# Two-layer graph network, first mixer's stage: GpSimd's row gathers issued in spells tied to TensorE's progress

## The reference

```python
xn = _layernorm(x, axis=-1)
x = x + _L0_gnn_ref(xn, sent_repr, src, dst, ...) + _L0_mix_ref(xn[None], W_qkv, W_out, b_out)[0]
```

## Time and profile before

| | us |
|---|---|
| timed executions | 2204.93, 2221.02, 2217.95 |
| median | 2217.95 |
| span of the profiled execution, first to last instruction | 2177.7 |
| median less span | 40.25 |

### The profile page before, as it was taken

How to read it: one execution, slowest core, us unless ns; L and a number is a source line. 1 busy time by engine, 2 the same in 40 slices (tenths; PEclk the granted TensorE clock), 3 DMA queues, 4 the chain that set the end, 5 groups by cost and what they waited for, 6 DMA issues and landing times. The chain is left out here.

```text
span 2177.7 us, 31463 instructions
## 1 busy us (share of the span) xinstructions
PE 1591.3 (73%) x7770; PEld 1251.9 (57%) x7770; DVE 1251.5 (57%) x3879; ACT 862.1 (40%) x2965; POOL 1067.5 (49%) x1173
## 2 busy tenths in 40 slices
PE   5635577766756786969999766877788887875892
PEld 4533444444444455959999654655566655664792
DVE  3523555555556687855777635454455455676435
ACT  2221656656555786635777431000011000143451
POOL 3751666666666500421222156666666666326351
PEclk8755668667777898989999867888888888896896
DMA  6741544444444302836555133333333333122786
GB/s 193 223 138 40 150 121 126 127 131 126 123 123 142 108 18 84 260 111 203 180 171 179 62 89 106 90 93 91 88 91 88 92 90 93 52 93 85 219 264 223
DMA packets 176882, 276.92 MB, mean 127 GB/s; under 512 B 28920, under 2 KB 132218, under 8 KB 176456
## 3 DMA queue, kind: packets, MB, share of 16 engines
q0 software_dynamic: 50352, 136.58, 21.8%
q1 hardware_dynamic: 82194, 94.23, 14.2%
q10 hardware_dynamic: 44166, 44.14, 6.1%
HBM read 202.35 MB, written 73.58 MB: 127 GB/s over the span
## 5 line engine op out<-in xcount | busy, mean ns | idle before, releaser
L501 POOL DMA_INDIRECT ring<-feat_d,src_lane x440 | 430.1, 977 | 281.8 <-issue 120.8
L1221 POOL DMA_INDIRECT rows<-xn_d,src_of x416 | 405.6, 975 | 228.7 <-issue 108.6
L1201 PE MATMUL bank<-ring,a_hot 128*128 128x260 f32 x880 | 318.9, 514 | 139.7 <-DVE ring L1100 81.4
L1392 PE MATMUL bank<-rows,big 128*128 x880 | 286.5, 443 | 129.1 <-DVE big L1300 68.9
L1130 ACT ACTIVATE ring<-ring 128x64 f32<-128x64 f32 x1540 | 375.3, 336 | 6.3 <-issue 5.6
L1201 PEld LDWEIGHTS bank<-ring,a_hot 128*128 128x128 f32 x880 | 207.5, 253 | 213.6 <-DVE ring L1100 95.7
L1309 DVE TENSOR_TENSOR big<-bank,big 128x256 f32 x440 | 186.7, 424 | 222.0 <-DMA m_bo<-in_L_mix_bo 114.7
L1392 PEld LDWEIGHTS bank<-rows,big 128*128 128x128 f32 x880 | 164.7, 209 | 225.9 <-issue 211.1
L1085 DVE TENSOR_TENSOR acc<-bank,acc 128x260 f32 x440 | 187.1, 425 | 143.2 <-DMA m_dst_bc<-dst_lo_d 60.9
L1362 ACT ACTIVATE big<-bank,a_col 128x256 f32<-128x256 f32 (+1 forms) x26 | 13.1, 552 | 416.9 <-PE bank L1407 177.5
L1300 DVE TENSOR_SCALAR big<-const,dst_lane,ew_lane 128x128 f32<-128x128 f32 x440 | 155.3, 353 | 1.0 <-PEq L95 1.0
(11 more groups left out here) (405 smaller groups left out, 2893.6 us busy)
## 6 DMA issues: line engine op xcount, KB each, us to landing
slots_d<-fold ACTq DMA_DIRECT2D x25, 1300.0 KB, 5.7
e_w_now<-in_L_ffn_w SPq DMA_DIRECT2D x56, 256.0 KB
a_dst_bc<-dst_lo_d SPq DMA_DIRECT2D x23, 512.0 KB
big<-in_L_ffn_W SPq DMA_DIRECT2D x16, 512.0 KB
e_x<-slots_d SPq DMA_DIRECT2D x56, 130.0 KB
ring<-feat_d,src_lane POOLq DMA_INDIRECT x440
rows<-xn_d,src_of POOLq DMA_INDIRECT x416
e_ys<-y_d SPq DMA_DIRECT2D x24, 256.0 KB
```

Of the source, the lines that this page charges most:

```text
L501: pool.indirect_dma_start(ring[:, q % RING, at, :], None, table, bass.IndirectOffsetOnAxis(ap=src_lane[:, n:n + 1], axis=0)).then_inc(gath ...
L1201: pe.matmul(bank[n % BANKS][:, 0:D + H], hot[:, q % HOTS, at, :], ring[:, q % RING, at, :], start=True, stop=True)\
L1221: pool.indirect_dma_start(rows[:, n % RING1, :], None, table, bass.IndirectOffsetOnAxis(ap=src_of[:, n:n + 1], axis=0)).then_inc(gathered[ ...
L1392: pe.matmul(bank[n % 4][:, 0:D], hot[:, n % HOTS, :], tile_of(rows, slots[n % 4]), start=True, stop=True)\
```

## The change

A constant `SPELL = 8` and two lines before each gather of the mixer's stage. The semaphore is `turned`, which TensorE increments once per tile of keys. GpSimd waits for `turned` to reach 5, 10, 15, 20 and 25 before gathers 47, 55, 63, 71 and 79; the first eight wait for nothing.

```diff
     L = 4
+    SPELL = 8
...
         def _(pool):
             for n in range(EARLY[NI + 1], BY_THEN):
+                spell = (n - EARLY[NI + 1]) // SPELL
+                if (n - EARLY[NI + 1]) % SPELL == 0:
+                    once(pool, turned, min(5 * spell, T))
                 gather_rows(pool, ring, gathered, src_lane, feat_d, n)
```

## The result

| us | before | changed | ratio, 95% interval |
|---|---|---|---|
| median of nine runs each | 2215.3 (2196.88 to 2223.58) | 2190.87 (2183.33 to 2203.45) | 0.9903, 0.9874 to 0.9931 |

The changed kernel is 24.4 us faster by the medians, a little over the 22.2 us named as the bound. The estimated ratio puts the gain at 0.97%, a little under 1%, and its interval, 0.69 to 1.26%, lies on both sides of the bound. That there is a gain is clear of noise; whether it is over or under 1% is not.

What follows compares the result with a forecast made beforehand. TensorE's signals held back by the gather stream were taken to bound the mixer's stage: 93.0 + 7.5 - 20 = 80.5 us in place of 95.0, a gain of 14.5 us from 2217.95 to 2203.5 us; range 2185 to 2226.

Steps and rivals of the forecast that it cites:

- What bounds the stage: Mixer's stage: what ends last is TensorE's signal, held back by the gather stream, 7 us and then 32 us late.
- The balance: Mixer's stage of 95.0 us split into parts; all work without gathers 50.2 us, 13.3 us of it done beside them.
- All five will hold: GpSimd's five waits in the mixer's stage would each really wait; the wait instructions themselves were costed at nothing.
- L: Mixer's stage: time after a spell of gathers until TensorE's signals come, taken as 1.5 us, five times.
- V: Mixer's stage: work done beside a spell of 10 us, taken as 5 us, counted for spells 1 to 4.
- the 8 us of spell 0: Work done beside the first eight gathers of the mixer's stage: the 4.6 us start and two tiles, about 8 us.
- the piece of eight: Eight gathers in the stage before the mixer's: 5.6 us of work beside 10 us of gathers, signals 1.5 us after.
- No gain: Rival, mixer's stage: V stays 1.25 us and L is 1.5; stage 95.5 us, kernel 2218.5 us; chance 0.20.
- slower: Rival, pauses after spells: clearing takes 5.1 us each time, V 1.25; stage 113.5 us, kernel 2236.5 us; chance 0.10.
- All hidden: Rival, mixer's stage: signals never pile up, V 10, L 0, GpSimd bounds; stage 59.5 us, kernel 2182.5 us; chance 0.20.
- The rule of the Trainium skill on DMA and compute engines: DMA never contends with a compute engine; by it holding the mixer's gathers gives nothing, the time of the no-gain case.
- What follows the stage: After the mixer's stage: the next stage starts near 204.5 us in place of 218.98, and what follows is as long as before.

Runs made afterwards that it cites:

- r2_last: Kernel before, with GpSimd holding all 42 gathers of the mixer's stage until the last tile is turned; 2205.06 us, kernel before 2201.97.
- r3_none: Kernel before, with the 42 gathers of the mixer's stage issued at the start of the aggregate instead; 2224.22 us, kernel before 2201.97.
- r13_gaps: Kernel before, with two small GpSimd multiplications after each gather of the mixer's stage and no holds; 2200.57 us, kernel before 2221.98.
- r4_sync: As r3_none, with SyncE issuing 42 plain copies of the same size in the mixer's stage; 2207.18 us, kernel before 2201.97.
- r9_plain: As r3_none, with GpSimd issuing 42 plain copies of the same size in the mixer's stage, no holds; 2209.48 us, kernel before 2192.83.
- r14_after: The changed kernel once more, unaltered, in a later call, 4 runs; 2196.8 us, ratio 0.9899 to the kernel before.
- r5_spell4: Changed kernel with spells of 4 in place of 8, each held for 2.5 more tiles, 10 runs; 2170.88 us, ratio 0.9905 to the kernel before.
- r6_spell16: Changed kernel with spells of 16 in place of 8, each held for ten more tiles; 2167.25 us, kernel before 2192.83.
- r10_spell2: Changed kernel with spells of 2 in place of 8, each held for 1.25 more tiles; 2166.79 us, kernel before 2192.83.

## Why the prediction was right, and where its sizes were off

**What bounds the stage: right.** That TensorE's signals are held back by the run of gathers was read from three timeline pairs and is now shown from both sides. Moved away (`r2_last`, `r3_none`), spaced (`r13_gaps`), or replaced by plain copies (`r4_sync`, `r9_plain`), the lateness is gone; with the run in place it is 32 us, twice, at the same tile.

**The balance.** "All the work, without gathers beside it" was put at 50.2 us and is 53.3 (`r3_none`). The 1.52 us per tile came from tiles 7 to 24, the last nine of which have no target numbers to turn (the list of target blocks has 16 entries; "the first 18 tiles" ahead of the prediction is wrong). In `r3_none` tiles 7 to 24 take 1.52 us each as well (142.94 to 168.79), but the seven before them 1.96 (129.24 to 142.94), which is the missing 3.1 us.

**The holds.** "All five will hold" was wrong: four did. The check was made for the first hold alone, and at before's pace, in which two tiles were turned when gather 47 could start. At the fourth hold, which asks for 20, the changed kernel had 22. The pauses of 3 to 8 us came out at 3.5 to 4.8, and 15.4 us in all.

**L, 1.5 us: right in size.** The last copy that was late came 1.6, 2.0, 1.5 and 3.1 us after a spell's end, 8.2 in all for 7.5. The first signal could come sooner (after spell 1 ScalarE had a copy at 151.76, 1.0 us after the end), so part of that time was worked. The 3.1 followed the double spell, as 5.1 followed the run of 42.

**V, 5 us, and the 8 us of spell 0: the mis-sized terms.** By the prediction's own balance, with measured values, 73.7 = 0.6 + 49.2 (spells 0 to 4, of which two ran without a gap) + 8.2 + (53.3 - 8 - 4 V), V is 7.4. That is a remainder: it takes in whatever the other terms have wrong. The tiles say more, counted from the stage's start and held against `r3_none`, in which nothing is late. Tile 8, the last turned beside spell 1, is turned after 23.4 us (there 22.6), tile 14, just before the double spell, after 40.5 (33.5), tile 24 after 65.0 (44.6). So nearly all that was lost, was lost after the first two spells, which cost 0.8 us together. An estimate, made by matching TensorE's matmuls of the two timelines in order, gives the work done: 10.3 us by the end of spell 0 in place of 8, then 9.7, 7.4 and 8.0 beside spell 1, spell 2 and the double spell, and 9.5 in the 15.4 us of pauses. V is then 6.3 on average for 5, but between 9.7 and 4.0 for a single spell, which no run explains. With these, the sum is 0.6 + 49.2 + 5.9 of pauses without work + (53.3 - 10.3 - 25.1) = 73.6. I had taken a value just under the 5.6 us of the piece of eight, for the two signals that a tile needs; that caution was not called for. The second check of the balance is the length itself, 0.6 + 49.2 + 15.4 of pauses + 8.45 from gather 79 to the next stage (192.42 to 200.87) = 73.7.

**The rivals.** No gain and slower fell: 95.5 and 113.5 us of stage were priced, and no spell length gave over 75.5. All hidden, 59.5 us, was not reached: 14 us remain to it, which are the 15.4 us of the holds. The changed time itself, 2190.87, lies in the band that I had given to that rival (2182 to 2192); of the 12.6 us to the forecast 6.8 are the stage, 2.7 the median of before (2215.3 by nine runs, 2217.95 by the first three), and the remaining 3 us are scatter, which is luck. By its stage and its pauses it is the forecast's case. The rule of the Trainium skill on DMA and compute engines, by which the prediction priced the time as unchanged, agrees with the plain copies (`r4_sync`, `r9_plain`: 0.4 us late at most); with this kernel's gathers, 32.3 us, the measurement decides against what was drawn from it.

**What follows the stage: as predicted, within what the profiles can tell.** The first aggregate took 627.3, 637.6 and 638.3 us behind a stage without spells (both profiles of before, `r2_last`) and 639.6, 641.4, 636.8, 629.7 and 634.9 behind one with spells (after, `r14_after`, `r5_spell4`, `r6_spell16`, `r10_spell2`), on average 634.4 and 636.5. The untouched second aggregate of the same traces has 624.4 and 624.9. Whether some 2 us are given back there stays open.

## What to carry to other kernels

Where an engine waits long and the profile names a releaser that was done long ago, look in the timeline for the instruction it really awaited: if that one ended long before too, the wait is for the news and not for the work, and moving the suspected stream behind a wait (here one line, `r2_last`) shows it. A run of indirect gathers that seems to overlap with work may overlap with nothing; a hold every few gathers, or two small instructions of GpSimd's after each, gave back 19 to 27 us of 95 here. Compare stages, not spans, of single profiles: two profiles of one kernel had spans 20 us apart and a stage equal to 0.02 us. Even a stage scatters once it has holds in it: by 3 us with spells of 8 and 5 us with spells of 4.

## What the runs showed of the hardware

- TensorE's signals to ScalarE and VectorE arrived up to 32.9 us late while GpSimd issued indirect gathers of 128 rows every 1.255 us, with gaps of 0.30 us. The operations themselves were not slower (turning a tile took 0.42 us in both). Once the gathers had ended ScalarE went on 1.0 to 5.1 us later. In the first 6.6 us of a run no signal was late (`r2_last`). ScalarE's and VectorE's signals to TensorE were not late inside a run (0.14 us).
- It is neither DMA traffic (373 GB/s, nothing late) nor GpSimd's DMA issue (one plain copy in 0.53 us, nothing late). Two multiplications of 0.21 us between gathers, start to start 1.6 us, took the lateness from 32.3 us to 0.4. I had not expected so little to be enough. Whether it is the gap, the pace or the kind of instruction in it wasn't told apart; what inside the chip does it stays open.
- A further gather costs 1.4 to 1.5 us in the first aggregate (42 more of them made it 58 and 64 us longer in two runs, with a scatter of 10 us) and 0.4 to 0.5 us in spells of eight beside the mixer's work (20.4 and 17.6 us over the 53.3 without any).
- Not tried: one small instruction after each gather in place of two, here and in the two aggregates, which have 359 gathers in the first alone. It is the open lead.
